# Far samples searched on GpSimd instead of VectorE, and the image moved in eight strips, in a windowed-attention and deformable-convolution kernel

## The chip, the cores and the metric

One core of one Trainium2 chip. The time is device microseconds of one execution, from launch to the last output byte. The program runs TensorE (PE, with its weight loads as PEld), VectorE (DVE), ScalarE (ACT), GpSimd (POOL) and the sync engine (SP), whose queue issues nearly all DMAs. GpSimd issues the indirect ones itself.

## The reference, cut to what matters

An image x of 2 x 128 x 128 x 128 floats (batch, channel, row, column) goes through two residual blocks:

```python
x = x + _L0_conv_ref(_gn(x), ...)   # windowed attention, 16 x 16 windows, 8 heads, then a projection
x = x + _L1_conv_ref(_gn(x), ...)   # deformable 3 x 3 sampling
```

The second block takes the group norm of x, computes a value image `v` and, for each pixel, each of G = 8 channel groups and each of K = 9 points, an offset (dx, dy) and a mask. Each point is sampled bilinearly, summed with its mask, and the sum is projected:

```python
loc_x = px + DIL * kx + off[..., 0] * OFFSET_SCALE
...
out = jnp.einsum('nhwkgc,nhwkg->nhwgc', sampled, mask_t)
out = out.reshape(N, L, C) @ output_proj_w.T + output_proj_b
```

Most offsets are at most 1 in size. A point whose offset is larger in x or y is called far here.

## The kernel before

The program has two parts. `attention` runs first and leaves its result in DRAM (`attended`); the change does not touch it. `deformable` then handles the two images of the batch one after the other (`b` = 0, 1), each in three stages.

Stage A, residual and statistics. The image is loaded into `x1` (128 channels x 16384 pixels, 8.39 MB). The load is four DMAs of a quarter each, and it waits until the output of the image before it is stored. GpSimd waits for all four and adds the projection bias in 32 pieces of 4 rows (L1059). For the same 32 pieces SP loads `attended` into `att` (256 KB each, two buffers, which are the first two slots of `vring`), PE multiplies with the projection weights into `sum_ps` (two buffers, L1205), and DVE adds the sum to `x1` (L1408) and takes `bn_stats` (L1410). A load into a buffer of `att` waits for the matmuls of two pieces before.

Stage V computes the value image and writes it, padded, to DRAM (`vals`).

The sampling stage runs over GROUPS = 32 groups of COLS = 4 image columns. Near points are handled densely: DVE makes tap weights (`tap_terms`, L1483 and L1488), PE turns them into `wt_ps`, DVE multiplies a 5 x 5 neighbourhood of columns with them (`products`, four per group, L1504), PE sums and transposes (L1265), and `result` (L1515) adds to `x1`. Neighbour columns come by DMA into an 8-slot ring `vring`; SP loads a column once the products of an earlier one are done.

Far points are taken out of the dense path and added one by one. LEAD = 6 groups ahead, ACT copies the offsets of a group to `off` and also takes their absolute value `size` (L1349, L1352). DVE's `find_far` works on them in three instructions: the larger of the two sizes (L1439), the masks with far points set to zero (`mf`, L1441, 288 numbers per partition and group), and keys of the far points (`keys`, L1444). Four groups are an epoch; there are eight per image. For the last group of an epoch DVE's `flags` finds the top eight keys per partition (L1455 and the small instructions after it), PE counts how many of the eight places are used by any partition, and `read_counts` writes that number to `rounds`. GpSimd then runs the far rounds of the epoch: each round looks up one far point per partition, gathers its corners by indirect DMA, and adds the result to DRAM (`far_sums`, L1131). An epoch's first GpSimd instruction is L1096, and `far_done` counts epochs done.

The order in each engine's queue is written by hand. In DVE's group body: products 0, result of two groups before, products 1, tap_terms of the next group, products 2, find_far of the group six ahead, flags if that group ends an epoch, products 3, read_counts. So the flags of epoch e are made in group 4e - 3 (for epoch 0, before the groups). In SP's group body, the third column of group q also waits for `far_done` of the epoch of q before it loads that group's `far_sums` (`load_far`), and the column loads behind it in SP's queue wait too. Storing the offsets of an epoch waits for `far_done` of two epochs before.

After the last group, SP stores `x1` in four DMAs of a quarter each.

Of the kernel before, what the change touches and what calls it, by code (L numbers as in the profile page):

```python
# [5 lines left out]
ALU = mybir.AluOpType  # L6
# [6 lines left out]
U16 = mybir.dt.uint16  # L13

B, C, H, W = 2, 128, 128, 128
PIX = H * W
# [43 lines left out]
HALVES = COLS // 2  # L60
TAP_W = TAPS * TAPS * G
# [662 lines left out]
def deformable(nc, x, attended, w_proj, bproj_row, w_value, bv_row, w_om, bom_row, w_out, b_out, vals, off_out, info_out, far_sums, out):  # L724
# [3 lines left out]
    with ExitStack() as ctx:  # L728
# [37 lines left out]
        att = vring[:, 0:2, 0:COLS * C].rearrange("p s (r c) -> p s r c", c=C)  # L766
        vrow = vring[:, 2:4, 0:COLS * C].rearrange("p s (r c) -> p s r c", c=C)
        off = sb("off", [P, RING_O, COLS, KG, 3])
        hat = sb("hat", [P, 3, COLS, 2 * KG])
        size = sb("size", [P, COLS, 2 * KG])  # L770
        reach = sb("reach", [P, COLS, KG])
        keytab = sb("keytab", [P, KE], U16)
# [40 lines left out]
        some_keys = sb("some_keys", [P, KI])  # L813
        rest = sb("d_rest", [P, KI])
        key_sum = sb("key_sum", [1, KI])
        key_left = sb("key_left", [1, KI], I32)
# [15 lines left out]
        x_in = sem("x_in")  # L832
        att_in = [sem("att_in0"), sem("att_in1")]
# [18 lines left out]
        size_ready = sem("size_ready")  # L852
# [19 lines left out]
        stored = sem("stored")  # L872
# [15 lines left out]
        QUARTER = PIX // 4  # L888
# [26 lines left out]
        def _(sp):  # L915
            start_counts(sp, counted)
            sp.sem_inc(off_stored, 16 * RING_O)
            for t, src in ((wproj_sb, w_proj), (wvalue_sb, w_value), (wom_sb, w_om), (wout_sb, w_out),
                           (bout_sb, b_out)):
                sp.dma_start(t[:], src).then_inc(w_in, 16)  # L920
# [13 lines left out]
            with sp.Fori(0, B) as b:  # L934

                sp.wait_ge(stored, count(64 * b))
                for n in range(4):
                    sp.dma_start(x1[:, n * QUARTER:(n + 1) * QUARTER],
                                 at(x, b * (C * PIX) + n * QUARTER, [[PIX, P], [1, QUARTER]])).then_inc(x_in, 16)
                with sp.Fori(0, NA // 2) as i:  # L940
                    for par in range(2):
                        a = b * NA + 2 * i + par
                        sp.wait_ge(a_done, count(a))
                        sp.sem_inc(sp_passed, 1)
                        sp.wait_ge(att_in[par], count(8 * (a - par)))
                        sp.sem_inc(sp_passed, 1)
                        sp.dma_start(att[:, par], at(attended, a * (COLS * W * C), [[C, P], [W * C, COLS], [1, C]])) \
                          .then_inc(att_in[par], 16)
# [57 lines left out]
                for n in range(4):  # L1006
                    sp.dma_start(at(out, b * (C * PIX) + n * QUARTER, [[PIX, P], [1, QUARTER]]),
                                 x1[:, n * QUARTER:(n + 1) * QUARTER]).then_inc(stored, 16)
            sp.wait_ge(stored, count(64 * B))

        @block.gpsimd
        def _(pool):
# [40 lines left out]
            with pool.Fori(0, B) as b:  # L1053
                pool.wait_ge(x_in, count(64 * (b + 1)))
                pool.sem_inc(pool_passed, 1)
                with pool.Fori(0, NA) as i:

                    rows = x1[:, bass.ds(i * (COLS * W), COLS * W)].rearrange("p (r w) -> p r w", w=W)
                    nc.gpsimd.tensor_tensor(rows, rows, bproj_sb[:].unsqueeze(1).to_broadcast([P, COLS, W]),  # L1059
                                            ALU.add).then_inc(b_added, 1)  # L1060
# [74 lines left out]
                def far_rest(e, slot):  # L1135

                    with pool.Fori(0, EPOCH) as u:
# [4 lines left out]
                        then(nc.gpsimd.tensor_reduce(key_sum[:], some_keys[:], AX.C, ALU.add))  # L1142
                        then(nc.gpsimd.tensor_copy(key_left[:], key_sum[:]))
# [12 lines left out]
                with pool.Fori(0, EPOCHS // RING_E) as i:  # L1156
                    for slot in range(RING_E):
                        e = RING_E * i + slot
                        pool.wait_ge(cnt_ready, count(b * EPOCHS + e + 1))
                        pool.sem_inc(pool_passed, 1)  # L1160
                        n_rounds = pool.value_load(rounds[0:1, slot:slot + 1], min_val=0, max_val=8)
                        with pool.If(n_rounds > 0):
                            pool.wait_ge(off_stored, count(16 * (b * GROUPS + EPOCH * (e + 1) + RING_O)))
                            pool.sem_inc(pool_passed, 1)
                            off_now[0] = off_out[slot]
                            restart()
                            epoch_base(e)
                            then(nc.gpsimd.tensor_copy(pos[:], far_at[:, slot, :, 0]))
                            look_up()
                            pool.sem_inc(scattered, 16)  # L1170
                            with pool.Fori(0, n_rounds) as t:
                                restart()

                                def look_ahead():
                                    then(nc.gpsimd.tensor_copy(pos[:].unsqueeze(2), far_at[:, slot, :, bass.ds(t + 1, 1)]))
                                    look_up()

                                far_round(far[:, slot, bass.ds(t, 1)], look_ahead)
                            pool.wait_ge(fetched, 32)
                            clear(fetched)  # L1180
                            with pool.If(n_rounds > 7):
                                far_rest(e, slot)
# [420 lines left out]
```

## Time and profile before

| | |
|---|---|
| median of 3 runs | 3431.49 us (3427.7 to 3433.02) |
| the profiled execution | 3429.93 us, span 3428.3 us |
| attention | to about 1573 us |
| image 0: load, stage A | 1580 to 1684 us |
| image 0: stage V and first offsets | to 1779 us |
| image 0: sampling groups | 1779 to 2496 us |
| store of image 0, load of image 1 | 2496 to 2542 us |
| image 1: stage A, stage V, first offsets | to 2721 us |
| image 1: sampling groups | 2721 to 3407 us |
| last store | to 3428 us |
| busy over the span | PE 81%, DVE 79%, ACT 55%, POOL 32% |

The busy shares are averages over stages with different limits, so the table says where each stage begins and ends, and the rows below say what goes on in it. The profiled execution stands within the three timed runs.

### The profile page before, as it was taken

What the parts mean: (1) busy time and instruction counts of PE and PEld (TensorE: products, weight loads), DVE (VectorE), ACT (ScalarE), POOL (GpSimd) and SP (SyncE); (2) the same over time, 40 slices, a digit from 0 to 9 for tenths busy, and PEclk for the clock granted to TensorE, in tenths of its full rate; (3) what the DMA queues carried; (4) which work ended last, traced back from release to release, by engine and by line L of the source; (5) the groups of instructions that cost most, each with busy time, mean ns of one, the idle gap of its engine ahead of it and who ended that gap; (6) DMA issues with size and microseconds to landing.
All of it is one profiled execution on the core that took longest, in us unless ns stands there. A gap on an engine that the chain in (4) does not pass through costs nothing.

```text
span 3428.3 us, 78376 instructions
## 1 busy us (share of the span) xinstructions
PE 2764.2 (81%) x22424; PEld 2218.6 (65%) x22424; DVE 2720.5 (79%) x6553; ACT 1881.8 (55%) x3529; POOL 1102.3 (32%) x1525
## 2 busy tenths in 40 slices
PE   0599999999999999993666999987936689989986
PEld 0365556565556565563556888887825578888886
DVE  5488888888888888883556999998924589999996
ACT  0488888888888888881262444332202634434331
POOL 0333333333333333324115321345231151114550
PEclk9999999999999999996798999998956999999998
DMA  6788888888888888884343333332263433333334
GB/s 219 126 140 142 142 140 143 137 142 142 142 140 142 137 142 142 141 129 152 102 137 82 99 99 97 99 101 81 87 241 100 135 103 100 97 98 98 103 87 161
DMA packets 348311, 432.45 MB, mean 126 GB/s; under 512 B 41968, under 2 KB 274816, under 8 KB 344048
## 3 DMA queue, kind: packets, MB, share of 16 engines
q1 hardware_dynamic: 336240, 423.85, 55.6%
q0 software_dynamic: 11904, 6.44, 1.6%
q8 instruction: 97, 1.59, 0.2%
q14 instruction: 70, 0.57, 0.1%
HBM read 283.33 MB, written 147.09 MB: 126 GB/s over the span
## 4 chain that ended last, share of the span: by engine, by line
DVE 21%; DMA 11%; issue 7%; PE 7%; POOL 4%; POOLq 1%; DVEq 1%; SPq 1%; ACT 1%; ACTq 0%
DVE prod L1504 13%; DMA vring<-attended 4%; DMA vring<-vals 3%; DVE tt L1488 3%; DMA vals<-vring 2%; PE sum_ps L1265 2%; PE sum_ps L1205 2%; DVE x L1515 2%; DMA o_sel<-off_out,pos 1%; POOL gath L1081 1%; PE wt_ps L1243 1%; DVE my L1483 1%; POOLq L1088 1%; DVE vring L1428 1%; PE om_ps L1228 1%
## 5 line engine op out<-in xcount | busy, mean ns | idle before, releaser
L585 ACT ACTIVATE prob<-sbias,nmax 128x256 f32<-128x256 f32 x2048 | 904.8, 501 | 196.2 <-DVE nmax L672 194.1
L1504 DVE TENSOR_TENSOR prod<-vring,wt_ps 128x1920 f32<-128x1920 f32 (+3 forms) x512 | 903.1, 1817 | 57.7 <-DMA vring<-vals 49.1
L672 DVE CUSTOM_DVE_ANT_0 sbias<-s_ps,nbias 128x256 f32<-128x256 f32 x2048 | 766.6, 420 | 224.8 <-PE s_ps L477 212.4
L1265 PE MATMUL sum_ps<-d_ident,prod 128*128 128x128 f32 x6400 | 759.2, 276 | 23.0 <-DVE prod L1504 23.0
L490 PE MATMUL pt_ps<-a_ident,prob 128*128 128x128 f32 x4096 | 644.5, 280 | 133.9 <-ACT prob L585 131.2
L1265 PEld LDWEIGHTS sum_ps<-d_ident,prod 128*128 128x128 f32 x6400 | 723.2, 143 | 37.5 <-DVE prod L1504 30.5
L490 PEld LDWEIGHTS pt_ps<-a_ident,prob 128*128 128x128 f32 x4096 | 447.6, 140 | 277.5 <-DVE probT L681 118.4
L477 PE MATMUL s_ps<-stack 96*128 96x256 bf16 x2048 | 396.4, 275 | 9.8 <-DMA stack<-parts_dram 9.8
L681 DVE COPY probT<-pt_ps 128x512 f32<-128x512 f32 x512 | 351.6, 687 | 11.7 <-PE pt_ps L490 11.7
L421 POOL CAST parts<-qk 128x1024 bf16<-128x1024 f32 x64 | 66.3, 1036 | 860.4 <-ACT qk L578 860.4
L1243 PE MATMUL wt_ps<-tt,d_ident 128*128 128x144 f32 x2304 | 319.8, 296 | 0.0
L1371 ACT COPY ssum<-sum_ps 128x512 f32<-128x512 f32 x64 | 37.5, 587 | 513.6 <-PE sum_ps L1275 513.6
L1243 PEld LDWEIGHTS wt_ps<-tt,d_ident 128*128 128x128 f32 x2304 | 314.0, 199 | 0.9
L477 PEld LDWEIGHTS s_ps<-stack 96*128 96x128 bf16 x2048 | 174.9, 98 | 203.7 <-issue 137.0
L592 ACT COPY probT<-pt_ps 128x512 f32<-128x512 f32 x512 | 290.4, 567 | 0.0
L1096 POOL COPY first_e<-first_at 128x2 f32 x16 | 2.8, 178 | 855.7 <-issue 578.1
L505 PE MATMUL o_ps<-probT,va 128*32 128x256 f32 x4096 | 274.1, 385 | 0.9 <-DVE probT L681 0.9
L1358 ACT ACTIVATE hat<-off,one_col 128x576 f32<-128x576 f32 x128 | 140.3, 1096 | 194.5 <-DVE tt L1488 194.5
L1205 PE MATMUL sum_ps<-wproj_sb,vring 128*128 128x128 f32 x512 | 118.3, 406 | 132.4 <-DMA vring<-attended 126.5
L1488 DVE TENSOR_TENSOR tt<-hat,my 128x864 f32<-128x864 f32 x192 | 192.9, 1060 | 9.8 <-DVE my L1483 1.0
L1205 PEld LDWEIGHTS sum_ps<-wproj_sb,vring 128*128 128x128 f32 x512 | 102.8, 299 | 148.4 <-issue 118.4
L672 DVE DVE_READ_ACCUMULATOR2_ANT nmax<- 128x1 f32 x2048 | 169.9, 83 | 0.0
(166 smaller groups left out, 3500.8 us busy)
## 6 DMA issues: line engine op xcount, KB each, us to landing
stack<-parts_dram SPq DMA_DIRECT2D x768, 128.0 KB, 7.5
vring<-vals SPq DMA_DIRECT2D x270, 320.0 KB, 2.9
parts_dram<-parts SPq DMA_DIRECT2D x64, 768.0 KB, 6.6
off_out<-off SPq DMA_DIRECT2D x64, 432.0 KB, 3.5
strips<-x SPq DMA_DIRECT2D x68, 256.0 KB, 3.5
a_stats_in<-x SPq DMA_DIRECT2D x16, 1024.0 KB, 4.9
far_sums<-nothing SPq DMA_DIRECT2D x64, 256.0 KB, 2.1
attended<-on SPq DMA_DIRECT2D x256, 64.0 KB
```

The lines of the kernel that those rows point to most:

```text
L477: mm = nc.tensor.matmul(s_ps[:, n % 2, half, :], stack[:, par, 0, h, at:at + P], stack[:, par, 1, h, w * NT:(w + 1) * NT], start=True, sto ...
L490: mm = nc.tensor.transpose(pt_ps[:, T_BANK[n % 4], kh, half * P:(half + 1) * P], prob[:, n % 4, half, kh * P:(kh + 1) * P], ident[:])
L505: mm = nc.tensor.matmul(o_ps[32 * j:32 * j + VA, t * NT:(t + 1) * NT], va[:, par, 2 * w + kh, 4 * t + j, :], probT[:, (4 * k + j) % 8, kh, ...
L585: ins = nc.scalar.activation(prob[:, n % 4, half, :], sbias[:, n % SBIAS, half, :], ACT.Exp, bias=nmax[:, n % SBIAS, half:half + 1], scale ...
L592: nc.scalar.copy(probT[:, n % 8], pt_ps[:, T_BANK[n % 4]]).then_inc(t_read_a, 1)
L672: ins = nc.vector.tensor_tensor_reduce(out=sbias[:, n % SBIAS, half, :], in0=s_ps[:, n % 2, half, :], in1=nbias[:, h, half, :], scale=1.0, ...
L681: nc.vector.tensor_copy(probT[:, n % 8], pt_ps[:, T_BANK[n % 4]]).then_inc(t_read_v, 1)
L1205: mm = nc.tensor.matmul(sum_ps[:, par, r * W:(r + 1) * W], att[:, par, r, :], wproj_sb[:], start=True, stop=True)
L1243: mm = nc.tensor.matmul(acc[:, :, jx:jx + KS, jy * G:(jy + KS) * G], ident[:], tt[:, jx, jy, 2 * half:2 * half + 2].rearrange("p r (a k) - ...
L1265: mm = nc.tensor.matmul(sum_ps[:, par, r * H:(r + 1) * H], prod[:, r % 2, dx, dy * C:(dy + 1) * C], ident[:], start=(r + dx + dy == 0), st ...
L1488: ins = nc.vector.tensor_tensor(tt[:, jx], hat[:, jx, :, 0:KG].unsqueeze(1) .to_broadcast([P, 3, COLS, KG]), my[:], ALU.mult)
L1504: nc.vector.tensor_tensor(prod[:, r % 2, first:last].rearrange("p a (t c) -> p (a t) c", c=CG), vring[:, at:at + wide].rearrange("p a (t c ...
```

## The change

- `find_far` moves from DVE to GpSimd, as six instructions on `off` itself: square the offsets, test them against 1, multiply the two tests (`within`), turn that round (`beyond`), mask (`mf`), keys. ACT's `size` is gone. `keytab` becomes float.
- GpSimd's queue now has a group body: find_far of the group six ahead and, if that ends an epoch, the far rounds of that epoch (`far_epoch`). Before the groups it runs find_far of groups 0 to 5, then the far rounds of epoch 0. DVE's `flags` waits for GpSimd's find_far of the epoch's last group.
- `x1` is loaded and stored in STRIPS = 8 strips of 1.05 MB. A strip is loaded once the store of its half's strip is done; at most two loads and two stores are under way. The strips are loaded between the pieces of `attended`, and GpSimd's bias add waits only for its strip.
- `att` has ATTS = 4 buffers instead of two.

```diff
-        att = vring[:, 0:2, 0:COLS * C].rearrange("p s (r c) -> p s r c", c=C)
+        att = vring[:, 0:ATTS, 0:COLS * C].rearrange("p s (r c) -> p s r c", c=C)
...
+                load_strip(0, 0, 0)
+                load_strip(1, 1, 0)
+                with sp.Fori(0, STRIPS // 2 - 1) as i:
+                    for par in range(2):
+                        load_attended(2 * i + par)
+                        load_strip(2 * i + par + 2, par, i + 1)
+                for par in range(2):
+                    load_attended(STRIPS - 2 + par)
...
+                with sp.Fori(0, STRIPS // 2) as i:
+                    for par in range(2):
+                        n = 2 * i + par
+                        sp.wait_ge(stored[par], count(16 * (b * (STRIPS // 2) + i + STRIPS // 2)))
+                        sp.sem_inc(sp_passed, 1)
+                        sp.dma_start(at(out, b * (C * PIX) + n * STRIP, [[PIX, P], [1, STRIP]]),
+                                     x1[:, bass.ds(n * STRIP, STRIP)]).then_inc(stored[par], 16)
...
+                def find_far(s):
+
+                    n, u = b * GROUPS + s.q, s.place % EPOCH
+                    here = off[:, s.place].rearrange("p r k t -> p (r k) t")
+                    pool.wait_ge(off_ready, count(n + 1))
+                    pool.sem_inc(pool_passed, 1)
+                    restart()
+                    then(nc.gpsimd.tensor_tensor(square[:], here[:, :, 0:2], here[:, :, 0:2], ALU.mult))
+                    then(nc.gpsimd.tensor_scalar(square[:], square[:], 1.0, None, ALU.is_le))
+                    then(nc.gpsimd.tensor_tensor(within[:], square[:, :, 0], square[:, :, 1], ALU.mult))
+                    then(nc.gpsimd.tensor_scalar(beyond[:], within[:], -1.0, 1.0, ALU.mult, ALU.add))
+                    nc.gpsimd.tensor_tensor(mf[:, s.place].rearrange("p r k -> p (r k)"), within[:], here[:, :, 2],
+                                            ALU.mult).then_inc(det_step, 1)
+                    nc.gpsimd.tensor_tensor(keys[:, s.epoch_slot(), u * KI:(u + 1) * KI], beyond[:],
+                                            keytab[:, u * KI:(u + 1) * KI], ALU.mult).then_inc(det_step, 1)
+                    pool.wait_ge(det_step, count(2 * n + 2))
...
+                def group(s):
+                    if s.has(LEAD):
+                        find_far(s.on(LEAD))
+                        if (s.place + LEAD) % EPOCH == EPOCH - 1:
+                            far_epoch(s.on(LEAD))
+
+                for q in range(LEAD):
+                    find_far(first_spot(q))
+                far_epoch(first_spot(0))
+                each_group(pool, group)
...
-                    act.wait_ge(off_ready, count(n + 1))
-                    nc.scalar.activation(xy(size[:]), xy_off(s), ACT.Abs).then_inc(size_ready, 1)
...
-                    nc.vector.tensor_tensor(reach[:], size[:, :, 0:KG], size[:, :, KG:], ALU.max).then_inc(det_step, 1)
...
-                    dve.wait_ge(det_step, count(3 * (b * GROUPS + s.q) + 3))
+                    dve.wait_ge(far_done, count(n + 1))
+                    dve.wait_ge(det_step, count(2 * (b * GROUPS + s.q) + 2))
...
-                    if s.has(LEAD):
-                        find_far(s.on(LEAD))
```

## Rows read from the trace of the kernel before

**Rows 1.** Busy time by stretch: stage A of image 0, four sampling groups of image 0.

```profile
1603.00:1690.00 87.00, 57.47 (x258) 49.81 (x257) 47.30 (x78) 1.46 (x3) 38.08 (x32) 0.64 0.31 91
...
2168.00:2254.00 86.00, 78.65 (x634) 74.31 (x633) 84.35 (x75) 34.95 (x41) 35.20 (x71) 1.00 0.34 101
```

**Rows 2.** Timeline (start us, us, what), loads, first and last pieces, stores.

```profile
1579.64 1.96 SPq L938 DMA_DIRECT2D x<-x  x4
...
1602.60 3.47 PE L1205 MATMUL sum_ps<-wproj_sb,vring 128*128 128x128 f32 x16 [42.40 <-DMA vring<-attended]
...
1682.90 0.69 DVE L1410 BATCH_NORM_STATS2 d_bn<-x  x1
...
2495.84 3.98 SPq L1007 DMA_DIRECT2D out<-x  x4
...
2541.86 3.78 PE L1205 MATMUL sum_ps<-wproj_sb,vring 128*128 128x128 f32 x16 [47.42 <-DMA vring<-attended]
...
3406.84 3.07 SPq L1007 DMA_DIRECT2D out<-x  x4
```

**Rows 3.** Timeline, PE in stage A: two pieces back to back.

```profile
1619.66 4.14 PE L1205 MATMUL sum_ps<-wproj_sb,vring 128*128 128x128 f32 x16 [1.10 <-DMA vring<-attended]
```

**Rows 4.** DMA issues: count, size of one, median us from issue to landing.

```profile
a_stats_in<-x SPq DMA_DIRECT2D x16, 1024.0 KB, 4.9
...
vring<-attended SPq DMA_DIRECT2D x64, 256.0 KB, 2.8
```

**Rows 5.** Timeline, DVE: find_far between two products, then flags of a later group.

```profile
2248.62 0.45 DVE L1439 TENSOR_TENSOR reach<-size 128x288 f32<-128x288 f32 x1
...
2249.98 7.00 DVE L1504 TENSOR_TENSOR prod<-vring,wt_ps 128x1920 f32<-128x1920 f32 x4
...
2270.78 1.36 DVE L1455 MAX8 top<-keys 128x8 f32<-128x1152 f32 x1 [0.15 <-DVE keys L1444]
```

**Rows 6.** Timeline, GpSimd: first and last instructions of two epochs' far rounds, next starts.

```profile
2278.38 0.18 POOL L1096 COPY first_e<-first_at 128x2 f32 x1 [37.96 <-issue]
...
2357.47 1.65 POOL L1131 DMA_INDIRECT far_sums<-gval,sidx  x1 [0.28 <-POOL gval L1130]
...
2378.55 0.18 POOL L1096 COPY first_e<-first_at 128x2 f32 x1 [19.44 <-issue]
...
3117.74 0.18 POOL L1096 COPY first_e<-first_at 128x2 f32 x1 [67.09 <-issue]
...
3181.20 1.64 POOL L1131 DMA_INDIRECT far_sums<-gval,sidx  x1 [0.28 <-POOL gval L1130]
...
3203.92 0.18 POOL L1096 COPY first_e<-first_at 128x2 f32 x1 [21.08 <-issue]
```

**Rows 7.** One line's instructions: L1096, once per epoch (ns min/median/max, first, last).

```profile
L1096 POOL COPY first_e<-first_at x16: 177/177/184, 1778.9 to 3289.8; 128x2 f32 x16
```

**Rows 8.** Waits of DVE, sampling stage of image 0: total us, times, longest us.

```profile
DVE prod L1504 <- DMA vring<-vals: 40.3, 3, 24.9
```

**Rows 9.** Groups of GpSimd instructions by shape: busy us, mean ns of one.

```profile
L424 POOL TENSOR_TENSOR rest<-qk,parts 128x1024 f32<-128x1024 f32 x64 | 137.0, 2141 | 11.8 <-POOL parts L421 11.8
...
L412 POOL TENSOR_SCALAR xn<-xraw,a_gnp 128x512 f32<-128x512 f32 x64 | 49.2, 769 | 19.8 <-POOL a_gnp L405 19.8
...
L169 POOL TENSOR_SCALAR info<-info 16x144 f32<-16x144 f32 x1 | 0.6, 607 | 0.1
L1044 POOL TENSOR_TENSOR bom_lo<-bom_sb,bom_mid 128x216 bf16<-128x216 f32 x1 | 0.6, 592 | 0.1
```

**Rows 10.** Timeline, GpSimd in an early epoch: one round's index arithmetic.

```profile
1858.48 1.78 POOL L1110 TENSOR_SCALAR idxf<-low,i_sel 128x1 f32<-128x1 f32 x1
1860.37 0.27 POOL L1111 TENSOR_SCALAR idx<-low,idxf 128x1 int32<-128x1 f32 x1
```

**Rows 11.** Timeline, DVE at that moment, and all of L1488 (ns min/median/max).

```profile
1857.22 2.99 DVE L1488 TENSOR_TENSOR tt<-hat,my 128x864 f32<-128x864 f32 x3
...
L1488 DVE TENSOR_TENSOR tt<-hat,my x192: 1044/1053/1151, 1756.4 to 3377.6; 128x864 f32<-128x864 f32 x192
```

**Rows 12.** Timeline, ACT: the second copy of offsets of image 0.

```profile
1755.02 0.86 ACT L1349 COPY off<-om_ps 128x864 f32<-128x864 f32 x1
```

More of the change, by code:

```diff
@@ L812, in deformable @@
         sidx = sb("sidx", [P, 1], I32)
[L813 to L816, printed above, removed]
+        some_keys, rest = beyond, within
+        key_sum = sb("key_sum", [1, KI])[:]
+        key_left = square[0:1].rearrange("p k t -> p (k t)")[:, 0:KI].bitcast(I32)
         om_ps = ctx.enter_context(nc.psum_tensor("om_ps", [P, 2, 512], F32))
@@ L934, in _, with load_attended @@
             with sp.Fori(0, B) as b:
[L936 to L942, printed above, removed]
+                def load_attended(a, place):
+                    sp.wait_ge(a_done, count(a))
+                    sp.sem_inc(sp_passed, 1)
+                    sp.dma_start(att[:, place], at(attended, a * (COLS * W * C), [[C, P], [W * C, COLS], [1, C]])) \
+                      .then_inc(att_in[place], 16)
@@ L943, in _ @@
                         sp.wait_ge(a_done, count(a))
                         sp.sem_inc(sp_passed, 1)
[L945 to L948, printed above, removed]
+                        sp.dma_start(att[:, place], at(attended, a * (COLS * W * C), [[C, P], [W * C, COLS], [1, C]])) \
+                          .then_inc(att_in[place], 16)
@@ L1053, in _ @@
             with pool.Fori(0, B) as b:
[L1054 to L1060, printed above, removed]
+                with pool.Fori(0, STRIPS // 2) as i:
+                    for par in range(2):
+                        pool.wait_ge(x_in[par], count(16 * (b * (STRIPS // 2) + i + 1)))
+                        pool.sem_inc(pool_passed, 1)
+                        with pool.Fori(0, NA // STRIPS) as j:
+                            rows = x1[:, bass.ds(((2 * i + par) * (NA // STRIPS) + j) * (COLS * W), COLS * W)] \
+                                .rearrange("p (r w) -> p r w", w=W)
+                            nc.gpsimd.tensor_tensor(rows, rows, bproj_sb[:].unsqueeze(1).to_broadcast([P, COLS, W]),
+                                                    ALU.add).then_inc(b_added, 1)
                 steps, off_now = [0], [None]
@@ L1154, in far_rest @@
                                 far_round(is_far[:], lambda: None)
[L1156 to L1159, printed above, removed]
-                        pool.sem_inc(pool_passed, 1)
[L1161 to L1165, printed above, removed]
-                            restart()
[L1167 to L1182, printed above, removed]
-                            pool.wait_ge(scattered, 16)
-                            clear(scattered)
-                        pool.sem_inc(far_done, 1)
@@ L1193, in _ @@
             pe.wait_ge(bias_split, count(13))
-            for ahead in (a_done, v_done):
-                pe.sem_inc(ahead, 1)
+            pe.sem_inc(a_done, ATTS - 1)
+            pe.sem_inc(v_done, 1)
             pe.sem_inc(sum_done, 2 * 2)
@@ L1535, in group @@
                         read_counts(s.on(LEAD))
-                for q in range(LEAD):
-                    find_far(first_spot(q))
-                    if q == 0:
-                        tap_terms(first_spot(0))
-                    if q == EPOCH - 1:
-                        flags(first_spot(q))
+                tap_terms(first_spot(0))
+                flags(first_spot(EPOCH - 1))
                 read_counts(first_spot(0))
```

103 lines of the change are left out of this document (64 added, 39 removed).

## The prediction, made blind

> **What bounds the kernel now.** I read the page for the stages first, then busy time by stretch, then the timeline at the hand-offs, and last GpSimd's timeline through the sampling stages.
>
> In stage A no engine is full: of 87 us PE is busy 57 and DVE 47 [rows 1]. From the first matmul at 1602.6 to the last statistics at 1683.6 the 32 pieces take 81 us, 2.53 us each [rows 2]. DVE's work is 47.3 / 32 = 1.48 us a piece, PE's 4.14 / 2 = 2.07 us at the clock of that moment [rows 1, 3]. What closes the cycle is the two-buffer load: matmuls 2.07, then a load of 2.8 us [rows 4] plus some 0.2 for the hand-off is 5.1 us for two pieces. That is 2.53 each, as seen. Ahead of stage A is pure DMA: 23 us from the issue of x to the first matmul for image 0, and 46 us (store, then load) between the images; a last store of 21.5 us ends the run [rows 2].
>
> In the sampling stages DVE is full, 84.35 of 86 us in four ordinary groups, with PE close behind at 78.65 [rows 1]. But twice or three times an image DVE stands still, 40 us in image 0, the longest 24.9 [rows 8]. There GpSimd's far rounds are late: SP waits for them in its queue and the column loads behind it wait too. So GpSimd, 32% busy on average, is the limit in some epochs. The 16 epochs [rows 7] have, counted from each L1096 to its last L1131, these numbers of rounds: image 0: 3, 3, 1, 2, 1, 3, 5, 3; image 1: 2, 3, 1, 1, 1, 4, 4, 3. Their lengths L by the same count are about 20 us for one round, 34 for two, 48 to 55 for three, 65 for four, 80.7 for five (the last two of these in [rows 6]). An ordinary epoch has 86 us of room (3117.74 to 3203.92), the five-round one took 100.2 [rows 6].
>
> **Strips and four buffers.** First matmul of image 0: it now needs two strips and one `att` piece instead of the whole image. A 1 MB load lands in 4.9 us [rows 4]; the second strip adds 2.5 us (8.39 MB took about 20 us, so 1.05 MB is 2.5), the piece 0.6. I take 8 us after the issue instead of 23: 15 saved. Between the images the stores still have to run (20 us); the loads can follow the sixth store, so 31 us instead of 46: 15 saved. Together **-30**.
>
> Pace of stage A: four buffers allow (2.07 + 3.0) / 4 = 1.3 us a piece, so PE or DVE limits. Bounds: 1.48 (DVE) and 2.07 (PE at this clock; the granted clock here is 0.64, so between its two levels of 1.2 and 2.4 GHz). A strip of 2.5 us now stands in the queue ahead of every fourth load: 2.07 + 3.0 + 2.5 over four is 1.9, but only one load in four pays it. I take 1.7 us, so 32 x 1.7 + 2 = 56 us against 81: 25 an image, **-50** (bounds -26 to -62). GpSimd's bias add (38.08 us for 32, 1.2 each [rows 1]) stays below that pace.
>
> The last store with two strips under way: each strip 2.5 us, the next one's start partly uncovered: **+1.5** (0 to 5). Sum of this part: **-78.5**.
>
> **What leaves DVE and ACT.** find_far costs DVE 2249.98 - 2248.62 = 1.36 us a group [rows 5]. ACT's `size`, about 1 us a group, lies in ACT's idle time and is worth nothing, except about 1 us at each start. PE has 7 us of idle in 86 [rows 1], and DVE would save 5.4, so DVE stays just ahead as the limit. I take 1.15 instead of 1.36 for the contention told next: 4.6 us an ordinary epoch.
>
> **What GpSimd gets.** No row has these shapes on GpSimd. Two-input instructions: 592 ns at 216 and 2141 ns at 1024 numbers give 0.18 us + 1.92 ns each [rows 9]. One-input ones: 769 ns at 512, 0.18 us + 1.15 ns each. So: square (576) 1.29, test (576) 0.85, within (288) 0.73, beyond (288) 0.51, mf 0.73, keys 0.73: 4.84 us. Gaps between dependent instructions are about 0.1 (1858.48 + 1.78 to 1860.37 [rows 10]), with the waits 0.5 in all: 5.3 us is the low bound. The offsets are read with gaps (three numbers a point). The only gapped one-input row is L169: 607 ns for 144, 3 ns each instead of 1.15, 2.6 times. At that factor square and mf would cost 2.7 us more: 8 us is the high bound. L169 steps over 16 bytes and here pairs lie together, so I stay near the plain rows: **F = 5.8 us** a group.
>
> The GPSIMD Engine Reference of the Trainium skill (section on performance pitfalls) says reads with an inner step over 8 bytes cost about 2.9 instead of 1.9 cycles. By it, and as an estimate, only mf's input (12 bytes) pays, F would be 5.6, and the total 8 us lower.
>
> Port contention: while DVE ran tap_terms, with both inputs in SBUF, GpSimd's tiny instructions took up to 1.78 us instead of 0.27 [rows 10, 11]. The other way, DVE's L1488 was stretched from 1053 to at most 1151 ns by instructions of 0.2 us [rows 11]; one of 0.7 to 1.6 us can hold it longer. The offsets of a group are copied about when the group starts, and find_far then ends 8 to 9 us in, just as tap_terms begins. I charge 0.2 us a group, above.
>
> The Trainium skill's page SBUF — State Buffer (section Who interferes with whom) says that a DVE instruction with two SBUF inputs and a GpSimd one that reads SBUF exclude each other for their whole length. The trace agrees for GpSimd's side, by the 1.78 us.
>
> **The new wait.** GpSimd's queue holds far rounds of epoch e, then find_far of groups 4e+4 to 4e+7, then epoch e+1. DVE's flags for e+1 wait for the fourth of these. Behind flags stand products 3 and read_counts, and for these waits GpSimd's next epoch. So from start to start an epoch takes at least L + 1.7 (last DMA landed) + 4F + 7.6 (flags at 2270.78 to far start at 2278.38 [rows 5, 6]) + 0.2 = L + 32.7, plus 2 of contention where DVE is not yet at rest. It was max(86, L + 19.5) before (80.7 + 19.5 = 100.2), because only the SP wait bound. Without GpSimd in the way it is 86 - 4.6 = 81.4.
>
> - Short epochs (one or two rounds; three in each image after the start): 6 x -4.6 = -27.6.
> - Second epochs, L = 54.6 and 54.2: 89.3 and 88.9 against 85.7: +6.8.
> - Image 0, sixth, L = 48.1: 82.8 against 86.1: -3.3. Seventh, L = 80.7: 113.4 against 100.2: +13.2.
> - Image 1, sixth and seventh, L = 65.1 (3117.74 to 3182.84 [rows 6]) and 65.2: 99.8 and 99.9 against 86.2 and 85.9: +27.6.
> - The six groups after the last flags: 2 x 6 x -1.15 = -13.8.
> - The starts: find_far of groups 1 to 5 runs back to back from the second copy of offsets (1755.9, now 1 earlier [rows 12]): 1755 + 5 x 5.8 + 2 = 1786, against 1778.9 [rows 7]. Epoch 0 (49.8 us), two more find_far and 9.5 us (1.7 + 7.8) to land and flag give the next start at 1856.9 against 1848.9; image 1 the same way 8.1. +16.1.
>
> Sum of the sampling stages: **+19**. The work taken off DVE comes back as waits on GpSimd, in the five long epochs and at the starts. Each microsecond of F moves this by 6 x 4 + 2 x 7 = 38 us.
>
> **Sum.** -78.5 + 19 = -59.5 against the profiled 3429.93: 3370.4; with the median 1.6 higher than that execution, 3372.
>
> **Rivals.**
> 1. GpSimd's wait does not bite: the finds are done in its idle time and every epoch gains. Then it is -78.5 - 16 x 4.6 = -152, 3279. For it: GpSimd is idle two thirds of the time. Against: its queue order, find after rounds. 4 in 100.
> 2. find_far on GpSimd is dear, and the time ends above before. One mechanism: gapped reads (or lock-outs by DVE) put F at 8 us. Then +84 more, 3455. It decides from F = 5.8 + 59.5 / 38 = 7.4 us. For it L169; against it the plain rows. 8 in 100.
> 3. Stage A stays at its old pace, because strips delay the `attended` loads: -30 + 1.5 + 19 = -9.5, 3422. For it: load latency is what binds now. Against: loads were at 91 GB/s in this stage [rows 1], and the strips double this at most, where x alone ran at over 400. 8 in 100.
> 4. Contention and code as forecast: 80 in 100.
>
> **How the numbers follow.** The forecast's own bounds: F from 5.3 (-19) to 6.8 (+38), stage A from 1.48 to 2.07 us (-12 to +24). 3338 to 3420 holds those that go together and leaves out rivals 1 and 2, and half of 3, under 2 in 10. A change under 0.2% (7 us) is what this measurement can't tell from none. Faster: 0.04 + 0.80 + 0.08, less 0.04 for the forecast and rival 3 both going a little wrong, 0.88; same 0.04; slower, rival 2, 0.08.
>
> **What would show it.** After the change: first matmul about 1588, last statistics near 1644; L1205 starts 1.7 us apart; no DVE instruction of find_far; GpSimd's square near 1.5 us and the six together near 5.8; DVE's L1455 waiting for GpSimd in the second and in the long epochs, 15 to 30 us in the longest; starts of L1096 about 81 apart in short epochs, 100 and 113 in the long ones. Wrong if F is far from 5.8, if L1488 is much above 1053 ns, or if stage A's pace stays over 2.2 us.

## The result

The changed kernel takes 3398.83 us (median of 4 runs, 3395.08 to 3403.12) against 3429.72 us (4 runs, 3427.7 to 3433.02) before: a ratio of 0.9909, interval 0.9892 to 0.9927. It is 31 us faster; the forecast's sum was 59.5. Its profiled span is 3399.5 us.

The timeline of the changed kernel, PE's and SP's lines at the hand-offs (start us, busy us, what, and in brackets the idle time before it and what ended it):

```profile
1577.80 1.05 SPq L951 DMA_DIRECT2D x<-x  x2
...
1586.36 5.99 PE L1264 MATMUL sum_ps<-wproj_sb,vring 128*128 128x128 f32 x32 [28.43 <-DMA vring<-attended]
...
1601.63 4.33 PE L1264 MATMUL sum_ps<-wproj_sb,vring 128*128 128x128 f32 x24 [3.46 <-DMA vring<-attended]
...
1629.64 7.62 PE L1264 MATMUL sum_ps<-wproj_sb,vring 128*128 128x128 f32 x40 [2.94 <-DMA vring<-attended]
...
2469.70 18.58 SPq L1033 DMA_DIRECT2D out<-x  x8
...
3377.12 17.68 SPq L1033 DMA_DIRECT2D out<-x  x8
```

The first matmul comes at 1586.36 instead of 1602.60 [rows 2]. Of these 16 us, 1.8 are there before the stage begins (the load of x is issued at 1577.80 instead of 1579.64 [rows 2]). The last statistics of image 0 end at 1644.20; stage A of image 1 goes from a first matmul at 2502.51 to 2561.05. PE now works off four or eight pieces at a time and then waits 0.6 to 3.5 us for `attended`: after every four loads of `attended` a strip stands in the queue.

Busy time by stretch, changed kernel: stage A of both images, and an epoch of one round. The columns, here and in [rows 1], are the stretch, its length, the busy us of PE, PEld, DVE, ACT and GpSimd, the granted clock, the DMA share and GB/s:

```profile
1586.00:1644.00 58.00, 41.83 (x256) 37.87 (x256) 42.62 (x64) 0.00 (x0) 36.59 (x30) 0.84 0.78 245
2502.00:2561.00 59.00, 41.41 (x256) 37.25 (x256) 42.85 (x64) 0.00 (x0) 36.77 (x30) 0.85 0.76 242
1903.70:1985.30 81.60, 77.83 (x627) 73.58 (x626) 80.38 (x63) 30.67 (x36) 39.38 (x52) 0.99 0.33 102
```

The stretch of stage A moves 245 GB/s where it moved 91 [rows 1], since most of x is now loaded in it. PE needs 41.8 us for the matmuls that took 57.5, and the clock granted in the stretch is 0.84 instead of 0.64. In the sampling stage, the one-round epoch takes 81.6 us, with DVE busy for 80.4.

The six instructions on GpSimd in the changed kernel, by line (count, then least, median and longest ns, first and last start):

```profile
L1193 POOL TENSOR_TENSOR square<-off x64: 1135/1147/1470, 1709.0 to 3246.8; 128x576 f32<-128x576 f32 x64
...
L1194 POOL TENSOR_SCALAR square<-square x64: 1646/1648/2352, 1710.3 to 3248.0; 128x576 f32<-128x576 f32 x64
...
L1197 POOL TENSOR_TENSOR mf<-within,off x64: 853/884/1751, 1713.3 to 3251.0; 128x288 f32<-128x288 f32 x64
...
L1199 POOL TENSOR_TENSOR keys<-beyond,keytab x64: 784/802/1635, 1714.1 to 3251.8; 128x288 f32<-128x288 f32 x64
```

And its waits (us, times, longest):

```profile
DVE top L1495 <- POOL keys L1199: 105.0, 10, 18.6
...
PE sum_ps L1264 <- DMA vring<-attended: 83.4, 11, 34.8
DVE prod L1544 <- DMA vring<-vals: 68.0, 3, 31.6
```

DVE's `flags` (L1495, the L1455 of before) now waits ten times for GpSimd's `keys`, 105 us in all. No such wait was there before. The waits for `vring` behind late far rounds have grown too. The same view of the whole kernel before has:

```profile
DVE prod L1504 <- DMA vring<-vals: 49.1, 4, 24.9
```

So it is 68.0 us for 49.1 in the whole kernel, and in image 0, of which [rows 8] are, 49.6 for 40.3. PE's eleven waits for `attended` are mostly the two starts of stage A (28.4 and 34.8 of 83.4 us).

Where the time comes from, as differences of the profiled executions (after less before; the spans differ by 28.8 us):

| | forecast | measured |
|---|---|---|
| first matmul image 0, and between the images | -15, -15 | -16, -13 |
| stage A of both images | -50 | -48 (81 to 57.8, 83.5 to 58.5) |
| last store | +1.5 | +1.5 |
| **strips and buffers** | **-78.5** | **-76** |
| short epochs (six) | -27.6 | -15.6 |
| second epochs | +6.8 | -1.3 (85.0 and 85.0, from 85.6 and 85.7) |
| image 0, sixth and seventh | -3.3, +13.2 | -0.2 (85.9), +15.2 (115.4) |
| image 1, sixth and seventh | +27.6 | +27.7 (99.6, 100.2) |
| groups after the last flags | -13.8 | -1.4 |
| starts | +16.1 | +22.5 |
| **find on GpSimd** | **+19** | **+47** |

From first to last product the two images take 41 us more than before (720.9 and 710.5 for 710.3 and 679.8). DVE is busy 49 us less in these stretches, and idle 90 us more.

How the long epoch runs is best seen in GpSimd's timeline, changed kernel, from the last far round of the five-round epoch to the next one's first instruction, with DVE's lines of its two long waits there:

```profile
2237.23 0.18 POOL L1126 COPY first_e<-first_at 128x2 f32 x1 [7.70 <-issue]
...
2316.41 1.65 POOL L1161 DMA_INDIRECT far_sums<-gval,sidx  x1 [0.28 <-DMA o_sel<-off_out,pos]
2320.34 1.14 POOL L1193 TENSOR_TENSOR square<-off 128x576 f32<-128x576 f32 x1 [2.28 <-DMA far_sums<-gval,sidx]
2321.57 1.67 POOL L1194 TENSOR_SCALAR square<-square 128x576 f32<-128x576 f32 x1
2323.33 0.67 POOL L1195 TENSOR_TENSOR within<-square 128x288 f32<-128x288 f32 x1
2324.08 0.43 POOL L1196 TENSOR_SCALAR beyond<-within 128x288 f32<-128x288 f32 x1
2324.60 0.88 POOL L1197 TENSOR_TENSOR mf<-within,off 128x288 f32<-128x288 f32 x1
2325.44 0.80 POOL L1199 TENSOR_TENSOR keys<-beyond,keytab 128x288 f32<-128x288 f32 x1
2326.71 1.15 POOL L1193 TENSOR_TENSOR square<-off 128x576 f32<-128x576 f32 x1 [0.47 <-POOL keys L1199]
...
2344.40 0.79 POOL L1199 TENSOR_TENSOR keys<-beyond,keytab 128x288 f32<-128x288 f32 x1
2352.68 0.18 POOL L1126 COPY first_e<-first_at 128x2 f32<-128x2 f32 x1 [7.49 <-issue]
```

```profile
2324.39 3.55 DVE L1544 TENSOR_TENSOR prod<-vring,wt_ps 128x1280 f32<-128x1280 f32 x2 [17.96 <-DMA vring<-vals]
...
2345.34 1.36 DVE L1495 MAX8 top<-keys 128x8 f32<-128x1152 f32 x1 [17.40 <-POOL keys L1199]
```

The last `far_sums` ends at 2318.1. After 2.3 us it has landed, the four finds run back to back, 6.4 us each (2320.34 to 2326.71 is one) and 24.9 together, DVE has waited 17.4 us for the last of them, and 7.5 us later the next epoch starts. So the epoch is L = 80.8 (the rounds, to the end of the last indirect DMA) plus 34.6 us, where the forecast had 32.7 plus up to 2. Before this wait DVE stands still for 18.0 us until the late rounds let SP load columns, where it was 13.3 in the kernel before.

### The profile page after: what moved, and what is told of

It is laid out like the page before. It is cut to its first block, busy times and chain, and to the rows that moved or that the text cites. A ratio compares the mean times of both kernels' runs of the same rounds, so it can differ in the third digit from the quotient of the medians.

```text
span 3399.5 us, 78682 instructions
## 1 busy us (share of the span) xinstructions
PE 2735.1 (80%) x22424; PEld 2194.5 (65%) x22424; DVE 2655.7 (78%) x6361; ACT 1818.2 (53%) x3465; POOL 1471.2 (43%) x1909
## 4 chain that ended last, share of the span: by engine, by line
DVE 16%; POOL 13%; DMA 8%; issue 8%; PE 4%; POOLq 2%; DVEq 1%; SPq 1%; ACT 0%; ACTq 0%
DVE prod L1544 10%; DMA vals<-vring 2%; POOLq L1118 2%; POOL gath L1111 2%; DMA vring<-attended 2%; DVE tt L1528 2%; POOL square L1194 2%; DMA vring<-vals 2%; PE sum_ps L1324 1%; POOL square L1193 1%; DMA o_sel<-off_out,pos 1%; PE sum_ps L1264 1%; DVE x L1555 1%; POOL mf L1197 1%; PE wt_ps L1302 1%
## 5 line engine op out<-in xcount | busy, mean ns | idle before, releaser
L1324 PEld LDWEIGHTS sum_ps<-d_ident,prod 128*128 128x128 f32 x6400 | 727.4, 143 | 40.3 <-DVE prod L1544 32.6
L1528 DVE TENSOR_TENSOR tt<-hat,my 128x864 f32<-128x864 f32 x192 | 210.4, 1150 | 9.4 <-PE wt_ps L1302 1.7
L1193 POOL TENSOR_TENSOR square<-off 128x576 f32<-128x576 f32 x64 | 74.8, 1169 | 297.8 <-ACT off L1407 252.9
L1407 ACT COPY off<-om_ps 128x864 f32<-128x864 f32 x64 | 56.3, 879 | 208.3 <-PE om_ps L1287 200.7
L506 PEld LDWEIGHTS o_ps<-probT,va 128*32 128x32 f32 x4096 | 106.9, 109 | 87.8 <-issue 33.5
```

The lines of the kernel that those rows point to most:

```text
L506: mm = nc.tensor.matmul(o_ps[32 * j:32 * j + VA, t * NT:(t + 1) * NT], va[:, par, 2 * w + kh, 4 * t + j, :], probT[:, (4 * k + j) % 8, kh, ...
L1324: mm = nc.tensor.matmul(sum_ps[:, par, r * H:(r + 1) * H], prod[:, r % 2, dx, dy * C:(dy + 1) * C], ident[:], start=(r + dx + dy == 0), st ...
L1528: ins = nc.vector.tensor_tensor(tt[:, jx], hat[:, jx, :, 0:KG].unsqueeze(1) .to_broadcast([P, 3, COLS, KG]), my[:], ALU.mult)
```

## The experiments

Each ratio is against the kernel before, measured on the same chip at the same time.

**One part alone.** `strips_only` has the strips and the four buffers, and leaves find_far on DVE. `find_only` moves find_far and GpSimd's queue order, and keeps the quarters and two buffers.

> The strips and the four buffers alone; find_far stays on VectorE. If the two parts of the change add up, this is the changed kernel less what the move of find_far cost in the sampling stages (727.0 + 716.5 us there against 716.4 + 685.9 before, and about 6 us more at the starts): 3429 - 76 = 3353 us. Rival, that the strips and buffers gain nothing by themselves and the saving came from a freed VectorE: near 3429.

Measured: 3355.23 us (3350.85 to 3361.04), ratio 0.978 (0.9763 to 0.9796), as expected.

> find_far on GpSimd alone, with the old loads and stores. By the wait for GpSimd: 3429 + 47 = 3476 us, with epochs of 100 us where four rounds are run and 115 where five are. Rival, that work taken off VectorE is worth what it cost there (52 groups x 1.36 us): 3358.

Measured: 3475.47 us (3471.0 to 3478.47), ratio 1.0127 (1.011 to 1.0144); its three long epochs take 115.1, 100.4 and 100.2 us. Against the 3431.01 us of the kernel before beside them, the parts are worth -75.8 and +44.5, together -31.3, which is the whole. The parts add up, and the kernel without the move is faster than the one with it.

**A longer find.** `long_find` is the changed kernel with a second test of 576 numbers in each find. The first test has left ones and zeros there, so the second one changes nothing but the time.

```diff
                     then(nc.gpsimd.tensor_scalar(square[:], square[:], 1.0, None, ALU.is_le))
+                    then(nc.gpsimd.tensor_scalar(square[:], square[:], 0.5, None, ALU.is_gt))
```

> The changed kernel with one more one-input instruction over 576 numbers in each find_far (1.65 us and a gap, 1.73 us; the result is unchanged). By the queue order on GpSimd (four finds between the rounds of six long epochs, seven at each of two starts, 38 in all on the path): 3399 + 66 = 3465 us. Rival, that what counts is the time for which VectorE and GpSimd shut each other out: 64 groups x 1.7 us, of which at most a third falls on tap_terms: 3399 + 36 = 3435 us, with L1528's mean well above its present 1150 ns. Rival, that the find lies in GpSimd's idle time: 3399.

Measured: 3479.41 us (3475.58 to 3489.98), ratio 1.0151 (1.0133 to 1.0169), span 3473.9. GpSimd's timeline of this kernel, one find at the end of the five-round epoch:

```profile
2352.75 1.14 POOL L1193 TENSOR_TENSOR square<-off 128x576 f32<-128x576 f32 x1 [1.97 <-DMA far_sums<-gval,sidx]
2353.98 1.67 POOL L1194 TENSOR_SCALAR square<-square 128x576 f32<-128x576 f32 x1
2355.74 1.65 POOL L1195 TENSOR_SCALAR square<-square 128x576 f32<-128x576 f32 x1
...
2360.88 1.15 POOL L1193 TENSOR_TENSOR square<-off 128x576 f32<-128x576 f32 x1 [0.48 <-POOL keys L1200]
...
2392.11 0.18 POOL L1126 COPY first_e<-first_at 128x2 f32<-128x2 f32 x1 [7.50 <-issue]
```

A find is 1.74 us longer, and the kernel 74 (spans) to 81 us (medians). The forecast's slope of 38 us for each microsecond gives 66; measured, it is 43 to 46. The long epochs are 106.5, 107.1 and 122.2 us instead of 99.6, 100.2 and 115.4: 6.8 to 7.0 each, four times the 1.74. A theory in which the find is hidden gave 0, one in which only the meetings with DVE's tap_terms cost gave 36. So the finds stand on the path, four of them per long epoch.

**No far samples.** In these kernels the bound is so wide that no point counts as far. They leave the far samples out of the result, and no epoch has a round. `no_far_before` is the kernel before, `no_far_strips` the one with strips only, `no_far_after` the changed one:

```diff
-                    then(nc.gpsimd.tensor_scalar(square[:], square[:], 1.0, None, ALU.is_le))
+                    then(nc.gpsimd.tensor_scalar(square[:], square[:], 1e8, None, ALU.is_le))
```

and on DVE in the other two

```diff
-                    nc.vector.scalar_tensor_tensor(out=mf[:, s.place], in0=reach[:], scalar=1.0,
+                    nc.vector.scalar_tensor_tensor(out=mf[:, s.place], in0=reach[:], scalar=1e4,
```

and the same in the keys.

> The kernel before with a far limit that no offset passes, so that every point takes the dense path and no far round runs (far samples are left out of the result). Three stalls in image 0 and one in image 1, 49 us of VectorE in all, go, and two L1096-to-L1096 stretches go back to 86 us: 3429 - 50 = 3379.

> The kernel with strips and four buffers alone, with no far rounds (far samples left out). If the strips' gain has nothing to do with the rounds: 76 us under no_far_before, 3303.

> The changed kernel with no far rounds (far samples left out): GpSimd only searches and is never late. By the wait theory the move now pays: 52 groups x 1.36 us off VectorE, less the 20 us by which L1523 and L1528 are stretched, less 5 us at the starts: some 45 us under no_far_strips, 3258. Rival, that the shared port is what cost the gain: no better than no_far_strips.

Measured: 3379.28 (3374.94 to 3380.74, ratio 0.9851, 0.9827 to 0.9875), 3302.9 (3297.62 to 3307.97, ratio 0.9635, 0.9608 to 0.9661) and 3261.28 us (3255.4 to 3266.7, ratio 0.9512, 0.9485 to 0.9539). The strips are worth 76.4 again. The move of find_far is worth **-41.6** us when GpSimd has no rounds, and was +43.6 with them (3398.83 against 3355.23). From first to last product the stages take 668.2 and 668.3 us with find_far on DVE, 646.8 and 644.7 with it on GpSimd. The 22.5 us fall on the 26 groups of an image that run a find_far (groups 0 to 25), so it is 0.87 us for each of them, of the 1.36 us that DVE is relieved of.

Where the other 0.5 us goes can be read from the traces. Groups of DVE instructions, `no_far_before`, then `no_far_after` (busy us, mean ns):

```profile
L1488 DVE TENSOR_TENSOR tt<-hat,my 128x864 f32<-128x864 f32 x192 | 191.7, 1054 | 9.8 <-DVE my L1483 1.0 <-PE wt_ps L1243 0.5
...
L1483 DVE TENSOR_TENSOR my<-hat,mf 128x864 f32<-128x864 f32 x64 | 67.3, 1052 | 8.9 <-ACT hat L1362 8.9
```

```profile
L1528 DVE TENSOR_TENSOR tt<-hat,my 128x864 f32<-128x864 f32 x192 | 211.6, 1156 | 8.9 <-PE wt_ps L1302 1.2
...
L1523 DVE TENSOR_TENSOR my<-hat,mf 128x864 f32<-128x864 f32 x64 | 73.8, 1153 | 17.1 <-ACT hat L1419 17.1
```

These four instructions of a group's tap_terms, the same in both kernels, take 26 us more in the two images (192 x 102 ns and 64 x 101 ns), while the products take as long as before (464.4 us an image in both). Between the first and the last product it is 12 us an image, or 0.46 us for each of the 26 groups: that is nearly all of the 0.49 that is missing from 1.36.

The same code that is a gain of 42 us by itself costs 44 as soon as far rounds and finds share a queue.

**The meeting of the two engines avoided.** `no_far_apart` is `no_far_after` with finds that wait until DVE has ended the group's tap_terms. (The last find of an epoch does not.)

```diff
+                        if (s.place + LEAD) % EPOCH != EPOCH - 1:
+                            pool.wait_ge(tt_ready, count(b * GROUPS + s.q + 2))
+                            pool.sem_inc(pool_passed, 1)
                         find_far(s.on(LEAD))
```

> no_far_after with one more wait: GpSimd starts the find of a group (all but an epoch's last) only when VectorE has finished tap_terms of the current group, so that their instructions with two SBUF inputs don't meet (far samples are left out, as there). If the meeting costs: L1528 and L1523 lose three quarters of their 24 us of stretch, and the time falls by 15 us to 3246. Rival, that the stretch costs nothing since PE is the next limit: 3261.

Measured: 3248.31 us (3247.31 to 3249.11), ratio 0.9466 (0.9451 to 0.948): 13 us below `no_far_after` (16 by the ratios, since the two ran on different chips), as expected. Its tap_terms instructions are nearly back at their old length:

```profile
L1531 DVE TENSOR_TENSOR tt<-hat,my 128x864 f32<-128x864 f32 x192 | 197.1, 1082 | 10.0 <-PE wt_ps L1305 2.4
...
L1526 DVE TENSOR_TENSOR my<-hat,mf 128x864 f32<-128x864 f32 x64 | 71.2, 1112 | 18.7 <-ACT hat L1422 18.7
```

DVE's timeline of the changed kernel shows what this takes away, two groups of three `tap_terms` instructions, and GpSimd's lines at the same time:

```profile
2981.72 3.00 DVE L1528 TENSOR_TENSOR tt<-hat,my 128x864 f32<-128x864 f32 x3
...
3001.01 5.04 DVE L1528 TENSOR_TENSOR tt<-hat,my 128x864 f32<-128x864 f32 x3
```

```profile
3000.06 1.58 POOL L1197 TENSOR_TENSOR mf<-within,off 128x288 f32<-128x288 f32 x1
3001.60 1.61 POOL L1199 TENSOR_TENSOR keys<-beyond,keytab 128x288 f32<-128x288 f32 x1
```

Three instructions take 5.04 us together where another group's take 3.00, and `mf` and `keys` take 1.58 and 1.61 us where they take 0.88 and 0.80 undisturbed. DVE loses 2.0 us and GpSimd 1.5. Over the changed kernel, the page has, for the same line (count, busy us, mean ns, idle us before):

```profile
L1528 DVE TENSOR_TENSOR tt<-hat,my 128x864 f32<-128x864 f32 x192 | 210.4, 1150 | 9.4 <-PE wt_ps L1302 1.7
```

which against the median of 1053 ns is 192 x 0.097 = 19 us. The L1523 beside it adds 4 us (71.7 us for 67.8 before). That is the "L1488 much above 1053 ns" of the forecast's last paragraph, by 9%.

The Trainium skill's page SBUF — State Buffer (section Who interferes with whom) says that such instructions of the two engines exclude each other. These rows agree that each lengthens the other, now for DVE's side too.

**The same in the changed kernel.** `after_apart` has the edit above on the changed kernel.

> The changed kernel with the same wait. In the long epochs GpSimd comes late and finds the wait already fulfilled, so only the eight or nine short epochs gain, some 1 us a group: 3399 - 10 = 3389. Rival, that the wait delays the last find of an epoch and with it flags: 3399 or more.

Measured: 3406.87 us (3403.66 to 3409.42), ratio 0.9925 (0.991 to 0.9941). The gain of 10 us that was expected did not come. The kernel is 8 us above the changed one, as the rival of that expectation had it, though by the ratios, whose intervals overlap, it is 5.5.

The rival's reason, that the last find comes later, is not what the trace shows. Three epochs are longer, 90.3, 88.1 and 102.3 us where they were 85.9, 85.0 and 99.6. Their far rounds alone account for that: L is 52.5, 51.8 and 65.6 us where it was 49.0, 47.0 and 63.1. What comes after L (landing, finds, flags) is 37.8, 36.3 and 36.7 where it was 36.9, 38.0 and 36.5. In the longer rounds more of GpSimd's small instructions meet tap_terms: 14, 13 and 15 of them overlap it, where it was 9, 7 and 10. In the first of the three epochs, GpSimd's and DVE's lines of `after_apart`, and GpSimd's of the changed kernel:

```profile
2162.27 1.99 POOL L1140 TENSOR_SCALAR idxf<-low,i_sel 128x1 f32<-128x1 f32 x1
```

```profile
2162.18 3.00 DVE L1531 TENSOR_TENSOR tt<-hat,my 128x864 f32<-128x864 f32 x3
```

```profile
2158.39 0.26 POOL L1140 TENSOR_SCALAR idxf<-low,i_sel 128x1 f32<-128x1 f32 x1
```

Nor did the wait take the meetings away from DVE: the tap_terms instructions take 290.7 us in the whole kernel, where it was 292.5, and the six short epochs together are 3 us shorter. Why so little was won there was not tested.

**One find of four on GpSimd.** `one_on_gpsimd` has the strips, and GpSimd only searches the first group of an epoch. DVE does the other three, and only one find is left between the rounds of two epochs. (To make room, GpSimd's find writes `within` into `mf`, and DVE's writes `reach` into `size`.)

```diff
+ON_POOL = 1
...
+                        if (s.place + LEAD) % EPOCH < ON_POOL:
+                            find_far(s.on(LEAD))
...
+                    if u < ON_POOL:
+                        return
```

> Strips and four buffers, and of each epoch's four groups only the first is searched on GpSimd, the other three on VectorE as before. By the queue order a long epoch then needs L + 9.5 + 6.3 us, 81 with four rounds and 97 with five, which is below what VectorE and the sync queue need anyway; 14 groups in the loop save 1.36 us each, less 0.3 of contention: 15 us under the kernel with strips alone, 3338. Rival, contention or the extra waits eat it: equal to strips alone or above it.

Measured: 3351.32 us (3349.67 to 3355.98), ratio 0.977 (0.9754 to 0.9786), 4 below `strips_only`, whose interval it overlaps. DVE's timeline of it, two groups:

```profile
1901.84 3.00 DVE L1564 TENSOR_TENSOR tt<-hat,my 128x864 f32<-128x864 f32 x3
...
1921.42 3.89 DVE L1564 TENSOR_TENSOR tt<-hat,my 128x864 f32<-128x864 f32 x3 [0.49 <-DVE my L1559]
```

GpSimd's find began at 1917.17 and met the tap_terms of the second line. The group before it, in which DVE has no find, took 19.2 us; this one, with a find of DVE's own (1.4 us), took 21.8. So 1.2 us of the 1.4 that the one find on GpSimd gives are lost again here, and the kernel is 13 us above what was expected. `one_apart` has it wait for the tap_terms before it:

```diff
                         if (s.place + LEAD) % EPOCH < ON_POOL:
+                            pool.wait_ge(tt_ready, count(b * GROUPS + s.q + 3))
+                            pool.sem_inc(pool_passed, 1)
                             find_far(s.on(LEAD))
```

> one_on_gpsimd (3351.3) with the find on GpSimd held back until tap_terms two groups on is over. There VectorE won 1.37 us in the group without find and lost 1.2 in the next, where the find met tap_terms. Without the meeting 6 to 10 of the 14 epochs win 1.2 us: 3351 - 10 = 3341. Rival: no change, 3351.

Measured: 3348.24 us (3342.91 to 3352.86), ratio 0.9761 (0.9748 to 0.9774). It has the lowest median of the kernels with the full computation, 2.4% below the kernel before and 1.5% below the changed one. It was expected 7 us lower. Its interval overlaps those of `one_on_gpsimd` and `strips_only`, so of the three only this is sure: all beat both kernels.

**Strips and buffers apart.** `strips_two_buffers` has the strips with two `att` buffers, `four_buffers` the quarters with four.

```diff
-ATTS = 4
+ATTS = 2
```

> The kernel with strips alone, but with two attended buffers instead of four. The strips then give the earlier first matmul and the overlapped store and load (about 16 + 13 - 1.5 us), the pace of stage A stays at 2.5 us or gets worse behind the strips: 3429 - 28 = 3401, and 4 to 8 us more if each strip of 2.5 us delays a load. Rival, that the strips alone set the pace: 3353.

> Four attended buffers alone: image still loaded and stored in quarters with no overlap, find_far on VectorE. No strip stands in the queue during stage A, so its pace should be PE's or VectorE's (1.45 to 1.6 us a piece, the last statistics 48 to 52 us after the first matmul) and not the 1.8 seen behind strips; 2 x 30 us less: 3429 - 60 = 3369. Rival, that the loads' own latency sets the pace with four buffers too: 1.8 us a piece, 3380.

Measured: 3413.21 us (3411.72 to 3421.28), ratio 0.9958 (0.9941 to 0.9974), and 3366.06 us (3364.72 to 3368.41), ratio 0.9811 (0.9796 to 0.9827). PE's timeline of `strips_two_buffers`:

```profile
1586.48 3.59 PE L1237 MATMUL sum_ps<-wproj_sb,vring 128*128 128x128 f32 x16 [28.40 <-DMA vring<-attended]
...
1603.45 3.69 PE L1237 MATMUL sum_ps<-wproj_sb,vring 128*128 128x128 f32 x16 [1.29 <-DMA vring<-attended]
1610.89 3.78 PE L1237 MATMUL sum_ps<-wproj_sb,vring 128*128 128x128 f32 x16 [3.75 <-DMA vring<-attended]
```

and of `four_buffers`, its first and last pieces:

```profile
1606.48 5.66 PE L1204 MATMUL sum_ps<-wproj_sb,vring 128*128 128x128 f32 x32 [42.69 <-DMA vring<-attended]
...
1650.75 1.16 PE L1204 MATMUL sum_ps<-wproj_sb,vring 128*128 128x128 f32 x8 [0.36 <-DVE x L1407]
1652.18 1.16 PE L1204 MATMUL sum_ps<-wproj_sb,vring 128*128 128x128 f32 x8 [0.27 <-DVE x L1407]
```

A piece takes 2.84 us with strips and two buffers (1586.48 to 1677.39 for 32), 1.8 with both, 1.54 with four buffers alone (1606.48 to 1655.90), where PE waits for DVE and no longer for a load; 2.53 before [rows 2]. The granted clock goes with the pace. Stage A of image 0 by stretch, `strips_two_buffers`, then `four_buffers`:

```profile
1586.00:1677.00 91.00, 55.98 (x256) 50.70 (x256) 43.84 (x64) 0.00 (x0) 36.73 (x30) 0.64 0.50 157
```

```profile
1606.00:1656.00 50.00, 38.01 (x256) 32.30 (x256) 42.57 (x64) 0.00 (x0) 38.98 (x32) 0.96 0.56 159
```

The strips start the stage 16 us earlier and delay the loads of `attended` in it. Four buffers alone gave 64 us of the 76, the strips 12 on top, and without the buffers 14.

## Why the prediction was nearly right

The direction, the range (3338 to 3420) and the likeliest case held. The point was 27 us low. The text's two sums stand apart: strips and buffers were within 3 us in every term, and the sampling stages were off by 28 (+47 for +19). That the direction held is owed to the first sum. The part that the forecast argued most about, find_far on GpSimd, is a loss 2.5 times the size forecast, and three of its terms missed by 6 to 12 us one way and one by 8 the other.

- **The chain of waits** was right: L plus the landing, four finds and the flags. The long epochs of image 1 came out at 99.6 and 100.2 us for 99.8 and 99.9, and `long_find` moved them by four times its extra. Rival 1, a wait that doesn't bite, falls with this. The `no_far` pair shows that its direction would have been right but for the far rounds (-42 us for its -74).
- **The terms that failed, largest first.** "The six groups after the last flags: -13.8" measured -1.4. That step was an error in reading, not of size: the last six groups of an image (26 to 31) have no group six ahead of them and never ran find_far, so nothing was taken off there. It should have been 0.
- **"Short epochs: 6 x -4.6"** measured -15.6, or -2.6 each: 81.6, 81.9 and 84.2 us in image 0, 81.8, 83.3 and 87.2 in image 1. The best ones are where the forecast had them. The step that failed is "I charge 0.2 us a group" for contention. It measured 0.5 us a group without rounds, and 0.57 in these six epochs, where the tap_terms instructions take 115.1 us for 101.4 before. That is 13.7 of the 17.0 us by which they fall short of 24 x 1.36. In the one of 87.2 us DVE also waits 3.3 us for PE, at a granted clock of 0.96.
- **F = 5.8 us.** It is 5.9 by itself (undisturbed), and 6.4 from one find to the next when they run back to back. Of its parts the test is 1.65 us where one-input rows gave 0.85, `mf` 0.88 and `keys` 0.80 where 0.73 was put; `square` 1.15 for 1.29, `within` 0.67 and `beyond` 0.43 for 0.73 and 0.51. So in the long epoch L was as taken and the rest 34.6 instead of 32.7, and "seventh +13.2" measured +15.2. In the two long epochs of image 1 the same excess (36.5 and 35.6) was offset by an L of 63.1 and 64.6 where 65.1 and 65.2 were taken: they agree partly by luck. The sixth of image 0 missed by 3.1 us in the same way (0.9 of them its L), and the starts ("+16.1", measured +22.5) have seven finds each. The forecast set L169 aside because pairs lie together here; they do in L169 as well (columns 0 and 1 of rows of four). It was right to do so all the same: `square`, in pairs 12 bytes apart, took 1.15 us, less than the plain rows gave.
- **"Second epochs: +6.8"** measured -1.3, the other way, since their L fell from 54.6 and 54.2 to 48.6 and 47.0. L was taken over unchanged from before, and that step failed: by the traces, L goes with how many of the rounds' instructions meet tap_terms. The same 71 instructions of GpSimd were busy 40.5 and 40.3 us before, and 12 and 13 of them overlapped tap_terms; they are busy 35.7 and 34.1 us now, and 8 and 7 overlap it. The `idxf` of [rows 10] that took 1.78 us beside tap_terms took 0.26 in the changed kernel's second epoch. Beyond L these epochs take 36.4 and 38.0 us, like the other long ones.

  The ten kernels with far rounds agree: their 50 epochs of three rounds took 47.0 to 50.1 us where at most 10 of the 71 instructions overlapped tap_terms, and 51.6 to 54.6 where 11 or more did. No run moved the rounds on purpose, so this is read from traces and not tested.

The GPSIMD Engine Reference of the Trainium skill (section on performance pitfalls) has inputs with a step over 8 bytes at 2.9 cycles instead of 1.9 in programs for GpSimd's own cores, half as much again. Here `mf`, the one with the 12-byte step, took 853 ns at least. `keys`, of the same size without it, took 784 and `within`, with a step of 8 bytes, 665. So the measurement is 1.1 to 1.3 times and not 1.5, and the forecast did well not to rest on it.

- **Rival 3** (strips delay the loads) was right in mechanism: with two buffers it happens (2.84 us a piece), and with four it costs 0.26 us a piece (1.8 for 1.54). **Rival 2**, F of 7.4 or more, did not occur, but `long_find` is that case: with an F of 7.6 us it ends 48 us above the kernel before.

## What to carry to other kernels

An engine's busy share says nothing of the room between two hand-overs in its queue: ask what stands between the last piece of the old work and the thing that someone waits for, and multiply the new work by how many pieces lie there. Test a move to another engine by itself, since a bundled gain hides a loss: here -76 and +45 would have been read as -31. An engine's idle time can also be dear for its neighbour: price the instructions of the other engine that the moved work will meet, not only its own. Before counting a saving per iteration, look at which iterations run the code at all.

## What the runs showed of the hardware

- GpSimd's test against a constant (`is_le`, 576 floats) takes at least 1646 ns, more than the product of two inputs of the same size (1135).
- DVE instructions with two inputs in SBUF and GpSimd's instructions slow each other: three of 1.0 us took 5.04, GpSimd's 0.88 and 0.80 became 1.58 and 1.61. That took back 0.46 us of each 1.36 us moved off DVE (`no_far_after`), and keeping them apart was worth 13 us of 3261.
- Three far rounds, 71 instructions on GpSimd, took 47.0 to 50.1 us in the epochs where at most 10 of them overlapped DVE's tap_terms, and 51.6 to 54.6 us where 11 to 14 did (50 epochs in ten kernels).
- The granted clock of stage A was 0.64 with two buffers, where PE was busy 57.5 of 87 us, 0.84 with four and strips (41.8 of 58 us), and 0.96 with four alone (38.0 of 50 us), for the same 256 matmuls.
- Loads of 1.05 MB ahead of 256 KB loads in a queue made a piece 2.84 us instead of 2.53 with two buffers, and 1.8 instead of 1.54 with four.
